# Second self attention of a decoder: projections in halves, spread over the slots of the plan

## The reference

```python
def _L1_attn_ref(x, Wq, Wk, Wv, memory, memory_norm, memory_weight):
    # D_MODEL 512, N_QUERY 4, N_HEAD 8, D_HEAD 16, D_KV 128
    q = x @ Wq.T; k = x @ Wk.T; v = x @ Wv.T
    qh = q.reshape(b, s, N_QUERY, N_HEAD, D_HEAD)
    kh = k.reshape(b, s, N_HEAD, D_HEAD)
    vh = v.reshape(b, s, N_HEAD, D_HEAD)
    scores = jnp.einsum('bsqhd,bthd->bqhst', qh, kh) * scale
    probs = jax.nn.softmax(scores, axis=-1)
    a_dot = jnp.einsum('bqhst,bthd->bsqhd', probs, vh)
    sigma_q = jax.nn.elu(q.reshape(b, s, N_QUERY, D_KV))
    a_mem = sigma_q @ memory / (sigma_q @ memory_norm)
    w = jax.nn.sigmoid(memory_weight)
    out = a_dot * (1.0 - w) + a_mem * w
x = _layernorm(x + _L1_attn_ref(x, ...), axis=-1)
```

## Time and profile before

| | us |
|---|---|
| median of three runs | 2840.01 (2838.26 to 2840.66) |
| the profiled execution | 2836.32 |
| its span | 2834.5 |
| PE busy in the span | 2405.4 (85%) |
| DVE, ACT, POOL busy | 1236.4 (44%), 855.3 (30%), 709.5 (25%) |

### The profile page before, as it was taken

One profiled execution on the slowest core, in us unless ns is written; L12 is line 12 of the kernel. 1 busy time (PEld: TensorE's weight loads), 2 busy tenths in 40 slices (PEclk: granted clock), 3 DMA queues, 4 the chain that ended last, 5 costly groups with the idle time before them and its releaser, 6 DMA issues. The chain is left out here.

```text
span 2834.5 us, 37569 instructions
## 1 busy us (share of the span) xinstructions
PE 2405.4 (85%) x14496; PEld 1879.0 (66%) x14496; DVE 1236.4 (44%) x2784; ACT 855.3 (30%) x1295; POOL 709.5 (25%) x667
## 2 busy tenths in 40 slices
PE   6999999999975888789999996678777855999974
PEld 4989889889864666678887775555453644555542
DVE  2343443343454553531111233465555455567535
ACT  2222222222222434322111112344444222444332
POOL 2532332231302532024333001433332010121210
PEclk8999999999986978899999998797788976999986
DMA  4000000000006652101000000321220645534101
GB/s 175 20 8 12 27 19 9 12 19 9 1 1 135 130 107 55 49 30 53 15 30 0 1 1 27 53 45 32 40 47 16 212 119 110 120 89 94 44 8 60
DMA packets 91967, 144.10 MB, mean 51 GB/s; under 512 B 10864, under 2 KB 64752, under 8 KB 88816
## 3 DMA queue, kind: packets, MB, share of 16 engines
q1 hardware_dynamic: 91792, 141.71, 20.5%
HBM read 82.95 MB, written 17.30 MB: 35 GB/s over the span
## 5 line engine op out<-in xcount | busy, mean ns | idle before, releaser
L1183 PE MATMUL PS<-WH,bXH 128*128 128x512 f32 x512 | 201.6, 394 | 5.4 <-POOL WL L1460 5.4
L1183 PE MATMUL PS<-WL,bXH 128*128 128x512 f32 x512 | 200.8, 392 | 0.0
L1183 PE MATMUL PS<-WH,bXL 128*128 128x512 f32 x512 | 200.8, 392 | 0.0
L558 DVE TENSOR_TENSOR xN<-PS,xN 128x512 f32<-128x512 f32 x128 | 88.5, 692 | 227.7 <-PE PS L361 227.7
L1852 DVE TENSOR_REDUCE aM<-PS 128x4 f32<-128x1024 f32 x128 | 153.1, 1219 | 67.0 <-PE PS L1694 66.3
L1378 DVE SCALAR_TENSOR_TENSOR s<-s,cf,PS 128x256 f32<-128x256 f32 x112 | 53.9, 481 | 250.2 <-ACT s L1298 241.2
L330 PE MATMUL PS<-aXH,QKH 128*128 128x512 f32 x384 | 152.3, 397 | 0.0
L330 PE MATMUL PS<-aXH,QKL 128*128 128x512 f32 x384 | 149.6, 390 | 0.0
L330 PE MATMUL PS<-aXL,QKH 128*128 128x512 f32 x384 | 149.6, 389 | 0.0
L1798 ACT ACTIVATE aPT<-PS 128x1024 f32<-128x1024 f32 x128 | 128.7, 1025 | 68.2 <-PE PS L1714 67.7
L643 POOL TENSOR_TENSOR E<-E,DM 128x256 f32<-128x256 f32 x64 | 47.1, 736 | 392.5 <-ACT E L475 392.5
(11 more groups left out here) (429 smaller groups left out, 6383.6 us busy)
## 6 DMA issues: line engine op xcount, KB each, us to landing
ckr<-in_cS SPq DMA_DIRECT2D x48, 256.0 KB, 7.1
cqs<-cQH SPq DMA_DIRECT2D x64, 128.0 KB, 3.8
sg<-in_gu SPq DMA_DIRECT2D x8, 1024.0 KB, 5.0
aqs<-aQH SPq DMA_DIRECT2D x64, 128.0 KB, 4.0
xks<-zkH SPq DMA_DIRECT2D x16, 512.0 KB, 8.2
xqs<-xQH SPq DMA_DIRECT2D x64, 128.0 KB, 2.6
gQK<-in_Wqk SPq DMA_DIRECT2D x8, 768.0 KB, 4.3
V<-in_xT SPq DMA_DIRECT2D x4, 1024.0 KB, 6.0
```

The source lines that it names most:

```text
L558: e.tensor_tensor(xN[:, t, :], PS[:, b, :], xN[:, t, :], ALU.add).then_inc(o_add.sem, 1)
L1183: mm = e.matmul(PS[:, b, :], x[:, kc, 128 * t:128 * t + 128], w[:, kc, :], start=kc == 0 and i == 0, stop=kc == KC - 1 and i == 2)
```

## The change

The projections are cut into pieces of 128 output columns: *key*, *value* and *query* 0 and 1 of each attention are 12 products each, with a bank and a semaphore step of their own. ACT copies each query half by itself (256 columns, twice). POOL's QL, e1 and max work on both halves after the second, and so do the DMAs. *values* is now called *value_turn*. The tiles qr, e1 and sgm have two buffers, by j % 2, and the waits for them are for the use two attentions before. The pieces are placed anew: the preparation of an even attention begins 28 slots ahead of its base instead of 22, that of an odd one 28 instead of 19, and n1 to n4 are in four slots instead of three. Fin and the norm parts come behind the projection within a slot (order 7 instead of 5). In a batch the pieces beside the score products are now: 0 elu of the odd attention, 1 pv, 2 memory of the odd one, 3 fin, 4 rows and turn_hi, 5 pv and turn_lo, 6 key and n1, 7 value and n2, 8 query 0 of the even one and n3, 9 pv, value_turn and n4, 10 query 1 of the even one, 11 fin, 12 rows, elu of the even one and query 0 of the odd one, 13 pv, 14 query 1 of the odd one, 15 memory of the even one.

```diff
-        qr, e1, sgm = W("aqr", [128, 2, 256]), W("ae1", [128, 2, 256]), W("sgm", [128, 2, 256])
+        qr, e1, sgm = ([W(f"{n}{i}", [128, 2, 256]) for i in range(2)] for n in ("aqr", "ae", "sgm"))
...
-        for lead, what in (((22, "turn_hi"), (21, "turn_lo"), (20, "keys"), (18, "queries"), (17, "values"), (16, "elu"),
-                            (14, "memory")) if j % 2 == 0 else ((19, "queries"), (17, "elu"), (15, "memory"))):
-            put(base - lead, 6, what, j)
+        for lead, what, i in (((28, "turn_hi", 0), (27, "turn_lo", 0), (26, "key", 0), (25, "value", 0), (24, "query", 0),
+                               (23, "value_turn", 0), (22, "query", 1), (20, "elu", 0), (17, "memory", 0)) if j % 2 == 0 else
+                              ((28, "query", 0), (26, "query", 1), (24, "elu", 0), (22, "memory", 0))):
+            put(base - lead, 6, what, j, i)
...
-        for lag, what in ((11, "fin"), (13, "n1"), (14, "n2"), (15, "n3"), (15, "n4")):
-            put(base + lag, 5, what, j)
+        for lag, what in ((11, "fin"), (14, "n1"), (15, "n2"), (16, "n3"), (17, "n4")):
+            put(base + lag, 7, what, j)
...
-        elif what == "keys":
-            R.use(("keys", bt), 1, v_in.upto(bt + 1))
-        elif what == "queries":
-            R.use(("queries", j), 1, q_hi.upto(j + 1))
...
+        elif what == "key":
+            R.use(("key", bt), 1, k_lo.upto(bt + 1))
+        elif what == "value":
+            R.use(("value", bt), 1, v_in.upto(bt + 1))
+        elif what == "query":
+            R.use(("query", j, i), 1, q_hi.upto(2 * j + i + 1))
...
+        def project(m, b, y):
+            for kc in range(KC):
+                for k, (w, x) in enumerate(pair3((WH, XH[y]), (WL, XL[y]))):
+                    mm = e.matmul(PS[:, b, 0:256], w[:, kc, 128 * m:128 * m + 128], x[:, kc, :],
+                                  start=kc == 0 and k == 0, stop=kc == KC - 1 and k == 2)
...
-            elif what == "queries":
-                src = PS[:, rooms["queries", j][0], :].rearrange("p (a n) -> p a n", a=2)
+            elif what == "query":
+                src = PS[:, rooms["query", j, i][0], 0:256]
                 if j >= 2:
                     e.wait_ge(*in_q[(j - 2) % 4].upto(6 * ((j - 2) // 4 + 1)))
-                if j:
-                    e.wait_ge(*l_out.upto(j))
-                e.wait_ge(*q_mm.upto(j + 1))
-                e.activation(qr[:, :, :], src, ACTF.Copy).then_inc(q_raw.sem, 1)
-                e.activation(QH[j % 2][:, :, :], src, ACTF.Copy).then_inc(q_hi.sem, 1)
+                    e.wait_ge(*l_out.upto(j - 1))
+                e.wait_ge(*q_mm.upto(2 * j + i + 1))
+                e.activation(qr[j % 2][:, i, :], src, ACTF.Copy).then_inc(q_raw.sem, 1)
+                e.activation(QH[j % 2][:, i, :], src, ACTF.Copy).then_inc(q_hi.sem, 1)
...
-            if what == "queries":
-                if j:
-                    e.wait_ge(*e_mm.upto(j))
+            if what == "query" and i:
...
             elif what == "elu":
+                if j >= 2:
+                    e.wait_ge(*e_mm.upto(j - 1))
                 e.wait_ge(*l_max.upto(j + 1))
                 e.wait_ge(*l_exp.upto(j + 1))
-                e.tensor_tensor(sgm[:, :, :], e1[:, :, :], qr[:, :, :], ALU.add).then_inc(l_out.sem, 1)
+                e.tensor_tensor(sgm[j % 2][:, :, :], e1[j % 2][:, :, :], qr[j % 2][:, :, :], ALU.add).then_inc(l_out.sem, 1)
...
-            elif what == "queries":
+            elif what == "query" and i:
                 if j >= 4:
                     e.wait_ge(*t_mm.upto(8 * (j - 3)))
-                e.wait_ge(*q_hi.upto(j + 1))
+                e.wait_ge(*q_hi.upto(2 * j + 2))
```

More of the change, by code:

```diff
@@ L1650, in tensor @@
                 mm.then_inc(x_mm.sem, 1)
-            elif what == "keys":
-                b, left = rooms["keys", bt]
+            elif what == "key":
+                b, left = rooms["key", bt]
                 for w in left:
                     e.wait_ge(*w)
-                e.wait_ge(*w_hi.upto(3))
-                e.wait_ge(*w_lo.upto(3))
+                e.wait_ge(*w_hi.upto(2))
+                e.wait_ge(*w_lo.upto(2))
                 e.wait_ge(*x_lo.upto(bt + 1))
-                project((4, 5), b, x).then_inc(k_mm.sem, 1)
-            elif what == "queries":
-                b, left = rooms["queries", j]
+                project(4, b, x).then_inc(k_mm.sem, 1)
+            elif what == "value":
+                b, left = rooms["value", bt]
                 for w in left:
                     e.wait_ge(*w)
[L1663 to L1666, removed]
+                e.wait_ge(*w_lo.upto(3))
+                project(5, b, x).then_inc(u_mm.sem, 1)
+            elif what == "query":
+                b, left = rooms["query", j, i]
+                for w in left:
+                    e.wait_ge(*w)
+                e.wait_ge(*w_lo.upto(5 + 2 * (2 * mp + i)))
+                project(2 * mp + i, b, x).then_inc(q_mm.sem, 1)
+            elif what == "value_turn":
+                b, left = rooms["value_turn", bt]
                 for w in left:
@@ L1757, in scalar @@
                              ACTF.Copy).then_inc(x_hi.sem, 1)
-            elif what == "keys":
-                b = rooms["keys", bt][0]
+            elif what == "key":
+                b = rooms["key", bt][0]
                 if bt:
@@ L1829, in vector @@
                                 XH[x][:, :, :].bitcast(F32), ALU.subtract).then_inc(x_lo.sem, 1)
-            elif what == "keys":
-                b = rooms["keys", bt][0]
+            elif what == "key":
+                b = rooms["key", bt][0]
                 if bt:
                     e.wait_ge(*in_k[(bt - 1) % 3].upto(6 * ((bt - 1) // 3 + 1)))
-                    e.wait_ge(*v_mm.upto(bt))
                 e.wait_ge(*k_hi.upto(bt + 1))
                 e.tensor_tensor(KL[:, :], PS[:, b, 0:256], KH[:, :].bitcast(F32), ALU.subtract).then_inc(k_lo.sem, 1)
-                e.tensor_copy(vT[:, :], PS[:, b, 256:512]).then_inc(v_in.sem, 1)
+            elif what == "value":
+                if bt:
+                    e.wait_ge(*v_mm.upto(bt))
+                e.wait_ge(*u_mm.upto(bt + 1))
+                e.tensor_copy(vT[:, :], PS[:, rooms["value", bt][0], 0:256]).then_inc(v_in.sem, 1)
             elif what == "memory":
@@ L1934, in sync @@
             bt, z, y = j // 2, j % 4, (j // 2) % 3
-            if what == "keys":
+            if what == "key":
                 e.wait_ge(*k_hi.upto(bt + 1))
```

34 lines of the change are left out of this document (18 added, 16 removed).

## The result

The changed kernel takes 2761.1 us (2760.5 to 2762.0, four runs) against 2840.3 us for the kernel before in the same runs: a ratio of 0.972, with a 95% interval of 0.971 to 0.974. It is 79 us faster, where I had forecast 37.

What follows compares the result with a forecast made beforehand. No engine is full, so the order of work in slots was taken to bound the kernel; six batches gave -35 us and the last slots -2, from 2836.3 to 2799.3, plus 3.7 for the median: 2803, range 2778 to 2831.

Steps and rivals of the forecast that it cites:

- Sum of a batch: Second self attention, sixteen slots: 39.3 + 1.1 + 2.0 + 1.6, plus 1 for small waits, 45.0 us against 50.8.
- The count by slots: Each slot costs about the larger of its PE, DVE and ACT parts: 44.6 us a batch before, 39.3 after.
- The excess above it: Batch time in the trace beyond the slots' sum: 50.8 against 44.6 us, 6.2 before, shown as PE waits and lower clock.
- The clock: Behind the wait at the odd memory PE still runs at 0.50 through slots 2 to 4: +1.6 us a batch.
- the shortest wait ahead of a fall: On PE before the projection at 1947.67: a 0.84 us wait, with another soon before it, precedes a fall of clock.
- The chain of the memory term: From the odd query projection in slot 14 to memory in slot 2, through POOL's sum: PE waits 3 us, 2.0 uncounted.
- Halves: Query copies of 256 columns on ACT: +0.7 us a batch, lying beside PE; DVE's work doesn't change.
- k_lo's +1.1 us: Slot 6 on DVE: k_lo waits for the key piece and KH's copy, delaying the norm's first part by 1.1 us.
- DMA queue: Stacked-query and row DMAs on SP: priced at nothing; if not hidden, up to 2 us in a batch.
- Ends: Stage outside slots 0 to 95: start about 0, with scores some 7 us later; slots 96 to the end -2 us.
- the clock stays low: Small gaps on PE in most slots keep the lower level: about +55 us, 2895; chance 0.09.
- the gain is whole: POOL's chain is hidden and the clock at 1.00: 40.5 us a batch, 2774 in all; chance 0.15.

Runs made afterwards that it cites:

- norm_fill: The kernel before with the norm's four parts in slots 6 to 9 and 44 unread products a batch on PE: 2809.1 us, ratio 0.989.
- lead26: The changed kernel with all preparations two slots later: 2759.8 us, ratio 0.972.
- early_norm_fill: The kernel before with the even attention's preparations two slots earlier, the norm in slots 6 to 9 and 34 unread products a batch: 2804.0 us, ratio 0.987.
- before_fill: The kernel before with 44 unread products of 256 columns a batch added on PE, in slots 2 and 6 to 8: 2824.0 us, ratio 0.995.
- early_even_norm: The kernel before with the even attention's preparations two slots earlier and the norm's parts in slots 6 to 9: 2808.8 us, ratio 0.989.
- one_third: The changed kernel with 4 instead of 12 products in each projection piece, so the output lacks the low parts: 2743.8 us, ratio 0.965.
- memory_0: The changed kernel with the even attention's memory in slot 0, behind the odd elu, instead of slot 15: 2750.4 us, ratio 0.970.
- glued: The changed kernel with key and value in one slot and both query halves in one slot: 2757.6 us, ratio 0.972.
- best_glued: The changed kernel with even memory in slot 0, first two memory steps six slots later, key with value and both query halves sharing slots: 2742.4 us, ratio 0.966.
- best: The changed kernel with the even memory in slot 0 and the first two memory steps six slots later: 2742.7 us, ratio 0.966.
- lead22: The changed kernel with all preparations six slots later: 2819.1 us, ratio 0.993.
- single: The changed kernel with one buffer each for qr, e1 and sgm, and the waits this needs: 2790.6 us, ratio 0.984.

## Why the prediction was wrong

The direction held, and so did the term of 5.3 us a batch for the slots. The step that failed is the one called "Sum of a batch": on top of the count I added 5.7 us of waits and low clock, and the trace has 0.3.

- *The count by slots*, 44.6 and 39.3 us: the batch after is 39.6. The sum held for the change and for norm_fill, but by luck in part. Taken from each slot's turned product to the next, in the batches that ran at 1.00, slots 1, 2 and 7 took 0.8, 1.6 and 1.3 us more than counted, and slots 0, 6, 11, 12 and 15 took 0.9, 1.2, 0.6, 0.4 and 0.5 less. The count is a rule of thumb with errors of 1 to 2 us a batch, as lead26 and early_norm_fill show.
- *The excess above it*, 6.2 us before (6.9 over six batches), where I left 5.7 for the change: measured 0.3. I added PE's waits (1.1, 2.0, 1.0) to the larger parts of the slots. But the count holds idle time of PE already. Before, PE's idle time is 10.5 us a batch (63.3 / 6) and the count's is 11.1 (44.6 - 33.5): in the sum of a batch the waits are no excess. The excess is the clock: PE is busy 41.0 us a batch for 33.5 us of work, 7.5 more. After, the idle time is 3.8 us against 5.8 in the count, and busy is 35.9, 2.4 more than the work. That is the reading I should have made of the earlier trace rows. It is one of sums: slot by slot the waits do stand out (before, slots 2 and 3 took 8.2 us for 4.5 counted, slots 6 to 9 some 14.5 for 11.3, lower level included), and other slots were shorter. That these are shorter because a wait lets DVE and ACT catch up fits this, but no run here shows it.
- *The clock*: I kept a fall behind every memory step, +1.6 us a batch. It fell behind two of six, and behind two of the five waits in slot 8, for which I had no fall. The lower level adds 13 us to the busy time of slots 0 to 95 and added 43 before. That it can be lifted without any of the new places is shown by before_fill; that the change lifted it because no two neighbouring slots are without a piece is what early_even_norm and before_fill suggest. one_third fits: with shorter pieces in the same places the clock of slots 0 to 95 was 0.90, and the time fell all the same. Of my sign "the shortest wait ahead of a fall": that pair, of 0.5 to 0.6 and 0.84 us, comes six times before and had a fall behind four of them.
- *The chain of the memory term*: foreseen as a wait of 3 us, measured 1.97. The slot took 1.6 us more than counted, and memory_0's batch, with 0.8 us of the wait gone and nearly all of the lower level, is 2.1 us shorter, so the place was right.
- *Halves* and k_lo's +1.1 us: as a whole the halves neither cost nor give (glued, best_glued), with 0.6 us a batch for them in best and a longer start against them. The wait of k_lo is there, with 1.29 us of PE's in slot 8 behind it, but slots 6 and 7 together took 6.0 us, as counted (5.9).
- *DMA queue*, priced at nothing: right for the change. With 22 slots it would have been 4.4 us a batch (lead22).
- *The double buffers*: I said that they don't help at memory, which holds, and forgot to price what they save at ACT's copies: 30 to 33 us (single).
- *The norm in four slots*: 6 to 10 us in the change, 22 alone in the kernel before.
- *Ends*: the start was foreseen at 0 and measured +3.7. The scores began 6.6 us later, as foreseen (7), but the slots up to the first turned product took 27.2 us for 30.1, 2.9 less where I had 7.6: waits of 2.26, 1.88 and 1.06 us stand there, and a clock of 0.50 in part. The last slots were foreseen at -2 and measured -10.8: the count has -4.9, and I expected a low clock for pv, but the stretch had 0.92 for 0.83 before.
- *Rivals*: the first (the clock stays low) was wrong. The third (the gain is whole, 40.5 us a batch, 2774) is the one that happened, with its chance of 0.15, and even it fell 13 us short.

*The rule that speaks against it.* The Trainium skill ("TensorE: Matmul & The Clock Gate", section "A second HAM failure mode: psum-queue depth-cycling") ties clock oscillation to frequent micro-idles of PE between groups of matmuls. The trace after agrees in part. With waits of 0.2 to 2.0 us in every batch the clock fell four times behind them in slots 16 to 95, so it did oscillate; but most of the same waits had no fall behind them, and the clock was 0.94, so the first rival, which rested on that rule, was wrong. In early_even_norm the trace agrees: in slots with scores alone no wait was above 0.40 us, and the clock fell.

What stays open: how the 41 us of idle time divide among the new places of the pieces. In the kernel before, the norm's move and the fill together gave 30 us by the ratios (norm_fill), and 37 with the even attention's preparations two slots earlier (early_norm_fill), of 79. The rest came only with the pieces in their new places and the double buffers that these need; two slots later is as good, and six slots later is not.

## What to carry to other kernels

Where each slot costs the larger of its engines' parts, count the slots before and after and split the excess of the trace into PE's busy time over its work and PE's idle time over the count's. In the sum of a batch the waits were mostly in the count here, and the excess in busy time was the clock, most of which the more even order gave back on top of the slots. Weighting the busy time with the granted clock checks this: the same work must come to the same number. The double buffers paid only together with the leads that need them: undone in the change they cost 30 to 33 us, added alone they gave none. The cheapest large piece was to spread DVE's block of norm work, one part to a slot: 22 us.

## What the runs showed of the hardware

More work on PE made the kernel faster: 44 products a batch that nobody reads took the granted clock of the stretch from 0.82 to 0.96 and 12 us off the whole. Less work did the opposite to the clock: with two thirds of the projections left out it was 0.90 instead of 0.94. And the same wait of 1.97 us on PE, at the same place of a regular loop, was followed by the lower level two times in six, while the waits of 2.12 and 2.13 us of the kernel before were followed by it every time.
